# A four-layer attention and experts kernel: the keys and values of layers 1 to 3 made at the start of their own layer

## The reference

```python
x = x + tanh(g_xattn[0]) * attn0(layernorm(x), ctx)          # 16 heads, biases
x = x + tanh(g_ffn[0]) * experts0(layernorm(x))              # top 2 of 8, one shared expert
x = x + tanh(g_xattn[1]) * attn1(keys=layernorm(ctx), q=layernorm2(layernorm(x)))
x = x + tanh(g_ffn[1]) * experts1(x)                         # top 2, capacity 256 each
x = x + tanh(g_xattn[2]) * attn2(ctx, layernorm(x), mask)    # one 8x8 matrix for all heads
x = x + tanh(g_ffn[2]) * experts2(x)                         # top 2, two shared experts
x = x + tanh(g_xattn[3]) * attn3(layernorm(x), ctx)          # one head; v = ctx @ Wv + bv is key and value
x = x + tanh(g_ffn[3]) * experts3(x)                         # top 1
# the part that the change moves, for l = 0..3: it depends on ctx and weights alone, never on x
k = keys_l @ Wk_l (+ bias);  v = keys_l @ Wv_l (+ bias)
```

## Time and profile before

| | us |
|---|---|
| median of 3 runs (lowest, highest) | 743.3 (742.02, 744.25) |
| the profiled execution, its own time | 742.13 |
| its span in the trace | 740.4 |
| TensorE matmul busy | 569.6 (77% of the span) |
| VectorE busy | 398.0 (54%) |
| ScalarE busy | 299.6 (40%) |
| GpSimd busy | 311.0 (42%) |

### The profile page before, as it was taken

One profiled execution on the slowest core, in us unless ns is written; L12 is line 12 of the kernel. 1 busy time (PEld: TensorE's weight loads), 2 busy tenths in 40 slices (PEclk: granted clock), 3 DMA queues, 4 the chain that ended last, 5 costly groups with the idle time before them and its releaser, 6 DMA issues.

```text
span 740.4 us, 13161 instructions
## 1 busy us (share of the span) xinstructions
PE 569.6 (77%) x3722; PEld 459.7 (62%) x3722; DVE 398.0 (54%) x1567; ACT 299.6 (40%) x736; POOL 311.0 (42%) x428
## 2 busy tenths in 40 slices
PE   1798967299967888249991999977899987963991
PEld 1466754299934666239990456744699846753991
DVE  3465743388865876302226676524488674543443
ACT  3264523144425564214441555422244344422661
POOL 4111575456622117734552110674166611173442
PEclk9998857599996998569995899658999997555996
DMA  8990001223262001112215000112033140012214
GB/s 263 223 394 1 20 31 37 79 74 88 73 223 121 1 2 45 38 49 66 67 51 150 0 1 1 37 48 73 25 87 94 42 114 0 1 33 79 60 51 121
DMA packets 56070, 54.84 MB, mean 74 GB/s; under 512 B 8088, under 2 KB 50864, under 8 KB 54944
## 3 DMA queue, kind: packets, MB, share of 16 engines
q1 hardware_dynamic: 48160, 39.75, 18.4%
q0 software_dynamic: 7840, 14.25, 5.9%
HBM read 34.99 MB, written 20.86 MB: 75 GB/s over the span
## 4 chain that ended last, share of the span: by engine, by line
PE 59%; DVE 9%; issue 8%; POOL 8%; ACT 7%; DMA 3%; DVEq 3%; POOLq 0%; SPq 0%; ACTq 0%
PE bank L839 17%; PE bank L851 11%; PE bank L679 5%; POOL slots L547 4%; PE bank L666 4%; PE bank L794 3%; PE bank L811 3%; PE bank L796 3%; PE bank L827 2%; PE bank L628 2%; ACT xn L923 2%; DVE x L1450 2%; ACT pay L923 2%; POOL rstd L509 2%; DVE stat L1074 1%
## 5 line engine op out<-in xcount | busy, mean ns | idle before, releaser
L573 POOL DMA_INDIRECT result<-xn,row x133 | 130.9, 984 | 139.4 <-DVE row L1402 128.8
L547 POOL DMA_INDIRECT slots<-pay,pos x112 | 110.5, 987 | 58.4 <-issue 33.0
L839 PE MATMUL bank<-xnT,gat 128*128 128x128 f32 x808 | 111.4, 282 | 1.0 <-DVE gat L1411 1.0
L851 PE MATMUL bank<-w,hsh 128*128 (+1 forms) x752 | 106.6, 277 | 1.7 <-DVE hsh L1418 1.1
L839 PEld LDWEIGHTS bank<-xnT,gat 128*128 128x128 f32 x808 | 100.8, 196 | 2.8 <-ACT xnT L1013 1.3
L851 PEld LDWEIGHTS bank<-w,hsh 128*128 128x128 f32 x752 | 95.3, 193 | 2.4 <-issue 2.4
L504 POOL TENSOR_SCALAR shift<-mv 128x4 f32<-128x4 f32 (+1 forms) x33 | 8.0, 241 | 209.4 <-DVE mv L1077 203.9
L679 PEld LDWEIGHTS bank<-vblk,probT 128*128 128x128 f32 x384 | 51.5, 204 | 35.7 <-ACT probT L963 29.8
L679 PE MATMUL bank<-vblk,probT 128*128 128x36 f32 x384 | 53.8, 289 | 13.5 <-ACT probT L963 13.3
L1013 ACT COPY xnT<-bank 128x128 f32<-128x128 f32 x133 | 35.6, 269 | 66.7 <-PE bank L827 62.4
L827 PE MATMUL bank<-ident,xg 128*128 128x128 f32 x133 | 37.7, 285 | 30.7 <-DMA xg<-slots 30.7
(11 more groups left out here) (235 smaller groups left out, 1080.7 us busy)
## 6 DMA issues: line engine op xcount, KB each, us to landing
xg<-slots SPq DMA_DIRECT2D x133, 64.5 KB
w<-in_w SPq DMA_DIRECT2D x4, 2048.0 KB, 10.7
pay<-result SPq DMA_DIRECT2D x28, 256.0 KB, 4.8
w<-in_w SPq DMA_DIRECT2D x1, 2560.0 KB, 19.3
w<-in_w SPq DMA_DIRECT2D x1, 2304.0 KB, 14.7
result<-xn,row POOLq DMA_INDIRECT x133
slots<-zeros SPq DMA_DIRECT2D x1, 2064.0 KB, 27.4
slots<-pay,pos POOLq DMA_INDIRECT x112, 2.3
```

Of the source, the lines that this page charges most:

```text
L547: pool.indirect_dma_start(out=(slots1 if l == 1 else slots)[:, :], out_offset=bass.IndirectOffsetOnAxis(ap=pos[:, t, k:k + 1], axis=0), in ...
L573: pool.indirect_dma_start(out=result[:, :], out_offset=bass.IndirectOffsetOnAxis(ap=row[:, s % TURN:s % TURN + 1], axis=0), in_=ysb[:, s % ...
L839: last = pe.matmul(bank[2 + p][:, c * P:(c + 1) * P], weights[:, c * P:(c + 1) * P], xgT[:, p, :], start=True, stop=True)
L851: last = pe.matmul(bank[6 + k % 2][:, 0:D], hid[:, k % 2, c * P:(c + 1) * P], w2f[:, bass.ds(e * (nf * D) + c * D, D)], start=c == 0, stop ...
```

## The change

`next_context` and its entries in `AT` are gone. Each engine calls `context(l)` for layers 1 to 3 as the first thing of layer l, ahead of `walk(l)`. The products go to banks 0 and 1, which the expert loop has just left, not to 5 and 6, and the waits that guarded banks 5 and 6 are replaced by waits of the first transposes, scores and softmax of the layer. `blockw` is made behind layer 1's keys and values.

```diff
         AT = [dict(combine=-8, stats=-8, scale=-7, tokens=-6, context=-5, queries=-3.5, stats_r=7, scale_r=7,
                    tokens_r=10, logits=10, pick=11, ranks=12, scatter=12,
-                   place=13, next_context=18),
+                   place=13),
...
+        KEY_BANKS = [(5, 6), (0, 1), (0, 1), (0, 1)]
...
             def context(l, g=0):
                 src = ctxTn if l == 1 else ctxT
-                out = bank[5]
+                out, values = bank[KEY_BANKS[l][0]], bank[KEY_BANKS[l][1]]
...
                         keys = ctxR[:, 1 if l == 1 else 0, b].rearrange("p j k -> p (j k)")
-                        last = pe.matmul(bank[6][:, b * P:(b + 1) * P], keys, WV[l], start=True, stop=l != 0)
+                        last = pe.matmul(values[:, b * P:(b + 1) * P], keys, WV[l], start=True, stop=l != 0)
...
-            def next_context(l, g):
-                context(l + 1)
-
             def transpose_tokens(l, g):
+                if l and g == 0:
+                    pe.wait_ge(Z["c_kT"], l + 1)
                 pe.wait_ge(Z["a_sc"], g_at(l, g) + 1)
...
                     pe.wait_ge(Z["a_qT"], g_at(l, g) + 1)
-                    if N == 0:
-                        pe.wait_ge(Z["c_blk"], 1)
+                    if n == 0:
+                        pe.wait_ge(Z["c_blk"], l + 1)
...
                     if g == 0 and i == 0:
                         pe.wait_ge(ld_w[l], 32)
-                        pe.wait_ge(Z["c_blk"], l + 2)
...
             for l in range(LAYERS):
                 three = GROUPS if l == 3 else ()
                 at = AT[l]
+                if l:
+                    context(l)
                 walk(l, tile, [
                     (at["context"] if l == 0 else 0, (0,) if l == 0 else (), context),
-                    (at["next_context"] if l < 3 else 0, (0,) if l < 3 else (), next_context),
...
                     last.then_inc(Z["c_blk"], 1)
+                    if l == 1:
+                        dve.wait_ge(ld_heads, 16 * HEADS)
+                        for i in range(3):
+                            last = dve.tensor_tensor(blockw[:, i, :].rearrange("p (h e) -> p h e", h=HEADS),
...
+                        last.then_inc(blk_done, 1)
```

More of the change, by code:

```diff
@@ L272, in flamingo @@
                    tokens_r=10, logits=10, pick=11, ranks=12, scatter=12,
-                   place=13, next_context=18),
+                   place=13),
               dict(combine=-9, stats=-7.5, scale=-7, tokens=-4, queries=-3, stats_r=7,
-                   scale_r=8, tokens_r=10, logits=10, pick=11, ranks=11, scatter=11, place=12, next_context=18),
+                   scale_r=8, tokens_r=10, logits=10, pick=11, ranks=11, scatter=11, place=12),
               dict(combine=-9, stats=-7, scale=-6, tokens=-5, queries=-4, stats_r=7, scale_r=8, tokens_r=9,
-                   logits=10, pick=11, ranks=12, scatter=12, place=13, next_context=20),
+                   logits=10, pick=11, ranks=12, scatter=12, place=13),
               dict(combine=-11.5, stats=-11.5, scale=-6, tokens=-5, queries=-5, stats_r=4, scale_r=5, tokens_r=7,
                    logits=8, pick=9, ranks=9, place=10, scatter=11)]
+        KEY_BANKS = [(5, 6), (0, 1), (0, 1), (0, 1)]
         BANK_R = [(1, 1, 1), (1, 1, 1), (1, 1, 1), (1, 3, 5)]
@@ L602, in context @@
                         keys = ctxR[:, 1 if l == 1 else 0, b].rearrange("p j k -> p (j k)")
-                        last = pe.matmul(bank[6][:, b * P:(b + 1) * P], keys, WV[l], start=True, stop=l != 0)
+                        last = pe.matmul(values[:, b * P:(b + 1) * P], keys, WV[l], start=True, stop=l != 0)
                         if l == 0:
-                            last = pe.matmul(bank[6][:, b * P:(b + 1) * P], ones[:],
+                            last = pe.matmul(values[:, b * P:(b + 1) * P], ones[:],
                                              rows[0:1, R["bv0"]:R["bv0"] + P], start=False, stop=True)
@@ L608, in context @@
                     for b in range(B):
-                        pe.matmul(bank[6][0:KEYS, b * P:(b + 1) * P], src[:, b * KEYS:(b + 1) * KEYS], WV[l],
+                        pe.matmul(values[0:KEYS, b * P:(b + 1) * P], src[:, b * KEYS:(b + 1) * KEYS], WV[l],
                                   start=True, stop=False)
-                        last = pe.matmul(bank[6][0:KEYS, b * P:(b + 1) * P], ones[:, 0:KEYS],
+                        last = pe.matmul(values[0:KEYS, b * P:(b + 1) * P], ones[:, 0:KEYS],
                                          rows[0:1, R["bv3"]:R["bv3"] + P], start=False, stop=True)
                 last.then_inc(Z["c_v"], 1)
-            def next_context(l, g):
-                context(l + 1)
             def transpose_tokens(l, g):
+                if l and g == 0:
+                    pe.wait_ge(Z["c_kT"], l + 1)
                 pe.wait_ge(Z["a_sc"], g_at(l, g) + 1)
@@ L693, in scores3 @@
                 if g == 0:
+                    pe.wait_ge(Z["c_blk"], 4)
                     pe.wait_ge(Z["s_x"], 2 * NG)
@@ L894, in context @@
             def context(l, g=0):
-                src = bank[5]
+                src = bank[KEY_BANKS[l][0]]
                 if l == 0:
@@ L1138, in context @@
                     bias_rows(1, "bo2")
[L1139 to L1146, removed]
                 if l < 3:
```

13 lines of the change are left out of this document (4 added, 9 removed).

## The result

| | before | after |
|---|---|---|
| median of 4 runs, us (lowest, highest) | 742.69 (742.02, 744.25) | 752.44 (749.75, 753.22) |
| the profiled execution, its span | 742.13, 740.4 | 752.26, 750.5 |
| mean granted clock of TensorE | 0.84 | 0.84 |

The ratio is 1.0116, 95% interval 1.0084 to 1.0148, which is 8.6 us; the medians stand 9.8 us apart. The forecast was 749.2 in a range of 744.0 to 753.0: the result lies in the range, 0.6 us under its upper end, and outside the 747 to 751 that I had called the forecast's own.

The account below looks back on a forecast made before the run. No single queue was taken to bound the kernel; it depends on the stage. Terms -1.9 - 0.5 + 0 + 3.9 + 1.8 + 0 + 2.6 sum to +5.9 us: 748.0 profiled, 749.2 median, range 744.0 to 753.0 (8 in 10).

Parts of the forecast that it names:

- What bounds the kernel from layer 0 to 1: Layer 0 to 1: VectorE's key, value and `blockw` work delays the late products and the combining behind them, +3.9 us.
- the boundaries swallow the blocks: Rival at layer borders: loading results back bounds combining, both blocks vanish in waits; -2.4 us, 740.9 us, chance 8%.
- The clock falls in TensorE's wait: Layer 0 to 1: TensorE idles 2.8 us for the first product, then runs at half clock, +1.8 us.
- the clock stays up: Rival from layer 0 to 1: TensorE's idle time is too short to lower its clock; +4.1 us, 747.4 us, chance 18%.
- End of layer 0, -1.9: End of layer 0: without ten TensorE passes, group 3's logits, picks and places come 1.9 us earlier; bounds 0.4 to 3.7.
- my lower bound of 0.4: End of layer 0: gain of 0.4 us if only the first wait, that of group 2's scatters, shrinks.
- End of layer 1, -0.5: End of layer 1: group 2's scatters wait less, group 3 hangs on an unmoved root; -0.5 us, between -1.0 and 0.
- end of layer 2, 0: End of layer 2: TensorE's 5.21 us go, but what follows waits for GpSimd's root; gain 0 to 0.6 us, taken as 0.
- layer 1 to 2, 0: Layer 1 to 2: 3.25 us of keys, values and blocks fit in VectorE's 5.96 us wait for results; 0.
- Layer 2 to 3, +2.6: Layer 2 to 3: 18 TensorE passes ahead of gapless late parts take half of 5.21 us at clock 1.00; +2.6 us.

Follow-up runs that it names:

- later comparisons: The changed kernel, unaltered, run again beside the kernel before on the second and the third chip: ratios 1.0061 and 1.0069.

## Why the forecast held, and where it did not

*What bounds the kernel from layer 0 to 1*: right. Combining follows the fourth product and not a landing, VectorE's waits among the products did not take up the block, and +3.9 measured +3.8. The rival in which the boundaries swallow the blocks is dead for layers 1 and 3 and true for layer 2, where I had it.

*The clock falls in TensorE's wait*: right for the profiled execution, +1.8 against +1.7, but not for each. Behind the wait it fell in three of five traces; in the other two the rival in which the clock stays up came true, and there the wait was the 2.8 us of the forecast, not 2.42. Judging by the length of the idle time alone would have had it the wrong way round.

*End of layer 0, -1.9*: wrong, the term that failed. I wrote that group 3's transpose "stands on TensorE behind two shared parts" and that "the next gate is ScalarE's two gate values". It also needs bank 1, which TensorE shares with group 2's places, and these stand in VectorE's list behind the first shared product. I had seen that order for group 2's scatters and not asked who else waits for them: 0.4 us of the 2.14 passed to the transpose. Nor did I ask what group 3's own places stand behind: another shared part, so that nothing passed to its scatters (129.32 in both profiles), and with the transpose 3.3 us earlier at most 0.8 us passed. That the -0.3 of the table is near my lower bound of 0.4 is luck: the bound was group 2's wait, the -0.3 arises behind the last scatter.

*End of layer 1, -0.5, end of layer 2, 0, layer 1 to 2, 0*: right, each to 0.1 us.

*Layer 2 to 3, +2.6*: mechanism right, size short by 0.5. I halved the time of 18 passes with the clock; they took 5.21 us at 0.50 and 2.99 at 1.00, a factor of 1.74. By the starts of the rows the 16 narrow ones took 4.50 us and 2.67, 0.28 and 0.17 us a pass, so they scale in part (the 0.30 of the prediction charged the two wide ones too little; and the clock of that stretch, 0.50, is in the trace but not in the rows it names). The Trainium skill, "TensorE: Matmul & The Clock Gate", section "LDWEIGHTS (loading the stationary operand)", has a weight load cost by its columns; by that the narrow passes should be no dearer than wide ones, an estimate of 1.9 us for this term. The profile after disagrees again: 0.17 us a pass at clock 1.00, where a wide pass of L605 takes 0.11.

*What the sum left out*: the clock in stages that the change only shifts, +2.6 us in the profiled pair. The sum by measured stages without them is 5.1 - 0.2 - 0.5 + 3.1 = 7.5 us, or 1.010, between the 1.0116 and the 1.0061 and 1.0069 of the later comparisons. Without the fall of the clock behind TensorE's wait it is 5.8 us, 1.007 on the slower chips. For the profiled execution the forecast was 748.0 and it took 752.26. The 4.2 us between are the gain at the end of layer 0 that did not come (+1.6), the small matmuls (+0.5) and the clock (+2.6), less 0.5 in the remaining rows. The first of these is an error of reading; the clock's could not be read from the trace before, only allowed for in the range. That 752.44 lies inside it is partly luck: had the clock cost 0.6 us more, it would have lain outside with the same reading of the kernel.

## What to carry to other kernels

Price a move by what the moved instructions stand in front of, one border at a time: the same edit cost 3.8 us (5.5 with the clock) where an engine went straight into dependent work, 3 us where TensorE had no gap, and nothing where everyone waited for a transfer. Before booking a gain, list everything that the freed instruction still waits for, the buffer it writes into included, and what each later step of its chain stands behind in its own engine's list. And where an engine's clock falls behind idle times, compare stages by their offsets in several traces and the whole by many runs: the same kernel had the fall in one execution and not in another.

## What the runs showed of the hardware

The clock is decided by more than the pause and the work behind it. Four traces have the same pause of TensorE in walk 1, with 0.1 to 0.4 us of work in 1.7 to 2.0 us, and the same instructions around it: two kept 1.00, one fell for 3.4 us, one for 7. Behind the wait from layer 0 to 1 the clock fell in three traces with 2.42 or 2.43 us of idle time and stayed in two with 2.82 and 2.84. And a start from a long idle time got full clock after 3.8 us in one and 6.1 us in another, with the same matmuls. The runs of the kernel before on one chip spread over 11 us.

The same program takes 4 to 5% longer on two of the chips (the changed kernel 786 us against 752), at about the same mean clock (0.848 against 0.842). Fifty microseconds of experts 0 in the changed kernel, on the slower chip and in the first profile (busy share and count of each engine as in the earlier trace rows):

```profile
150.00:200.00 50.00, 44.18 (x368) 41.81 (x367) 32.55 (x111) 16.56 (x55) 27.23 (x28) 1.00 0.25 70
```
```profile
145.00:195.00 50.00, 49.81 (x427) 49.30 (x426) 38.88 (x127) 22.64 (x67) 30.07 (x30) 0.97 0.28 79
```

TensorE does 368 matmuls there instead of 427. It has four pauses of 0.7 to 1.5 us, each for a product of VectorE whose input from ScalarE came late. In the first, the matmuls that ScalarE needed ended at 154.8 and it started at 156.67, with nothing in the trace that it waits for:

```profile
153.71 1.06 PE L839 MATMUL bank<-xnT,gat 128*128 128x128 f32 x8
...
156.67 0.38 ACT L1015 ACTIVATE hsh<-bank 128x256 f32<-128x256 f32 x1 [1.95 <-PE bank L839]
```

What holds it is open. The instructions' own durations are nearly the same on both: a matmul of L839 takes 0.28 us on average in either.
